# Signalling each group's edge sums by a drain of TensorE instead of by the last matmul, in all four graph layers of a fused GNN and expert network

## The reference, cut to what matters

```python
msg = table[src] * norm[:, None]                          # one row per edge, gathered by src
agg = jax.ops.segment_sum(msg, dst, num_segments=6250)    # summed per target node
```

## Time and profile before

| | us |
|---|---|
| runs of the kernel before | 5611.9 and 5638.83, median 5625.36 |
| span of the profiled execution | 5647.3 |
| granted TensorE clock, mean over the span | 0.835 |
| TensorE matmul, busy | 4017.9 |
| VectorE, busy | 3072.1 |
| GpSimd, busy | 2967.7 |
| ScalarE, busy | 1485.5 |

### The profile page before, as it was taken

One profiled execution on the slowest core, in us unless ns is written; L12 is line 12 of the kernel. 1 busy time (PEld: TensorE's weight loads), 2 busy tenths in 40 slices (PEclk: granted clock), 3 DMA queues, 4 the chain that ended last, 5 costly groups with the idle time before them and its releaser, 6 DMA issues.

```text
span 5647.3 us, 64923 instructions
## 1 busy us (share of the span) xinstructions
PE 4017.9 (71%) x21108; PEld 3177.4 (56%) x21109; DVE 3072.1 (54%) x7978; ACT 1485.5 (26%) x4028; POOL 2967.7 (53%) x3232
## 2 busy tenths in 40 slices
PE   7764555555546676777778977788776778785999
PEld 6653433334335466666666755666655666664766
DVE  7765645555447655555555565555546554443434
ACT  6502322232232222222223322222231111124221
POOL 7736466666656555555640016555556555543233
PEclk9987777776678777777779988899988998997999
DMA  2423433333333222222221013333333332225231
GB/s 89 122 68 93 118 96 97 96 96 96 97 89 87 78 80 79 80 80 80 82 67 34 20 60 87 89 92 90 90 102 97 102 93 84 83 77 176 69 104 54
DMA packets 272106, 489.99 MB, mean 87 GB/s; under 512 B 85684, under 2 KB 176805, under 8 KB 271635
## 3 DMA queue, kind: packets, MB, share of 16 engines
q0 software_dynamic: 139312, 377.94, 23.8%
q1 hardware_dynamic: 125336, 101.03, 5.9%
q10 hardware_dynamic: 7118, 6.83, 0.4%
HBM read 426.41 MB, written 62.17 MB: 87 GB/s over the span
## 4 chain that ended last, share of the span: by engine, by line
PE 39%; another core or an unknown queue 23%; DVE 22%; issue 10%; ACT 3%; DVEq 2%; POOL 1%; DMA 1%; ACTq 0%; SPq 0%; POOLq 0%
PE PSA L1020 11%; PE PSA L1164 5%; DVE ACC L2016 4%; PE PSA L1411 4%; PE PSA L1397 4%; PE PSA L1173 3%; PE PSA L1298 3%; PE PSA L1314 3%; DVE XIN L1989 2%; DVE XT L1989 2%; PE PSA L985 1%; PE PSA L979 1%; DVE WORK L2282 1%; PE PSA L1149 1%
## 5 line engine op out<-in xcount | busy, mean ns | idle before, releaser
L853 POOL DMA_INDIRECT WORK<-tab,SRC x2632 | 2522.8, 958 | 2146.8 <-issue 768.0
L2016 DVE TENSOR_TENSOR ACC<-ACC,PSA 64x256 f32 x1360 | 568.9, 418 | 1457.7 <-remote 959.4
L1020 PE MATMUL PSA<-WORK,XIN 128*128 128x256 f32 x3192 | 960.0, 454 | 458.0 <-ACT XIN L1491 341.5
L1020 PEld LDWEIGHTS PSA<-WORK,XIN 128*128 128x128 f32 x3192 | 711.0, 233 | 612.1 <-issue 492.5
L1020 PE MATMUL PSA<-WORK,XT 128*128 128x256 f32 x2072 | 594.5, 437 | 161.4 <-ACT XT L1491 85.4
L1020 PEld LDWEIGHTS PSA<-WORK,XT 128*128 128x128 f32 x2072 | 439.4, 222 | 248.9 <-issue 172.6
L1149 PE MATMUL PSA<-WORK 128*128 128x256 bf16 x784 | 161.6, 290 | 327.4 <-DVE WORK L2282 98.2
L1173 PE MATMUL PSA<-WORK,XT 128*128 128x42 f32 x832 | 153.8, 350 | 211.8 <-DVE WORK L1989 211.7
L1149 PEld LDWEIGHTS PSA<-WORK 128*128 128x128 bf16 x784 | 69.4, 104 | 379.8 <-issue 230.4
L1989 DVE TENSOR_TENSOR XIN<-PSA,DST 128x512 f32<-128x512 f32 x412 | 279.1, 679 | 2.5 <-DVE PSA L2323 1.4
L1173 PEld LDWEIGHTS PSA<-WORK,XT 128*128 128x128 f32 x832 | 145.8, 260 | 223.7 <-DVE WORK L1989 221.7
(11 more groups left out here) (492 smaller groups left out, 6899.0 us busy)
## 6 DMA issues: line engine op xcount, KB each, us to landing
WORK<-tab,SRC POOLq DMA_INDIRECT x2632
ACC<-in_L_ffn_w SPq DMA_DIRECT2D x16, 1024.0 KB
tab<-WORK SPq DMA_DIRECT2D x98, 128.0 KB
slots_x<-FILL SPq DMA_DIRECT2D x4, 2080.0 KB
ACC<-slots_x SPq DMA_DIRECT2D x8, 910.0 KB
tab<-ACC SPq DMA_DIRECT2D x49, 128.0 KB
WORK<-tab SPq DMA_DIRECT2D x49, 128.0 KB
before_y<-X SPq DMA_DIRECT2D x7, 896.0 KB
```

What stands on the lines that cost most here:

```text
L853: po.indirect_dma_start(out=rows[:, 0:width], out_offset=None, in_=tab[:, :], in_offset=bass.IndirectOffsetOnAxis(ap=SRC[:, c:c + 1].bitca ...
L1020: last = pe.matmul(PS[h][:, 0:D], chosen[:, j * P:(j + 1) * P], rows[:, 0:D], start=(j == 0), stop=(j == Q - 1))
L2016: return ve.tensor_tensor(rows, rows, PS[h][half, 0:D], ALU.add)
```

## The change

TensorE's loop over the groups no longer puts the increment of `s_p` on the last matmul of the product. It issues a `drain` behind the product, and the drain increments `s_p`. It does so for every group of all four layers. The rest of the queue of TensorE follows behind the drain as before, and nothing changes on another engine.

```diff
@@ -1194,7 +1194,8 @@
                         pe.wait_ge(s_free, 4 + BEGIN[1] + g - 2)
                     if layer >= 2 and g >= 2:
                         pe.wait_ge(s_free, 4 + BEGIN[layer] + g - 1)
-                    product(SEL[g % NS], rows_of(layer, g), bank_of(layer, g)).then_inc(s_p, 1)
+                    product(SEL[g % NS], rows_of(layer, g), bank_of(layer, g))
+                    pe.drain().then_inc(s_p, 1)
                     if layer == 3:
                         gate_steps(g)
                     if g in early:
```

## The result

The kernel before took 5625.36 us, the changed one 5788.95 us (median of 2 runs each, 5777.82 and 5800.09). The ratio is 1.0294, 95% interval 1.0218 to 1.0371: slower. The profiled execution has a span of 5776.1 us, 128.8 us over that of before.

The account below looks back on a forecast made before the run. A cycle of gather streams and held TensorE completions was taken to bound the kernel. Drains, 128 us, plus the queue behind held drains, 80 us, made 208 us over the 5625 us median: about 5835 us, range 5740 to 6040.

Parts of the forecast that it names:

- What bounds the kernel: In the four layers, gathers set 5.0 us a group; GpSimd's pauses and layer starts add 809 us, to 4209 us.
- The cycle of rows of gathers and late completions: GpSimd streams gathers, TensorE's signals stay out, slots fill up, GpSimd pauses, signals come, GpSimd starts again.
- Case (a): On TensorE, the drain too waits for held completions: its signal is as late as the matmul's, and the queue stands behind it.
- rival 1: The drain's signal is prompt, or its flush lets held ones out; sums come earlier: 5330 us, chance 0.32.
- First term: TensorE's queue: 0.35 us per drain, 92 us in layers 2 and 3, 36 in layers 0 and 1; together 128 us.
- Second term: TensorE work behind a held drain starts after release: 0.6 us per pause in layers 2 and 3, 80 us.
- Pauses: GpSimd's pauses keep their length, near 2.8 us in layers 2 and 3, but are more in number.
- rival 3: Far slower: each burst gives back one group only, one pause per group in layers 2 and 3: 6200 us, chance 0.08.
- Rival 2: No change: what the drain keeps back would have stood still anyway; drains cost some 40 us, 5665 us, chance 0.20.

Follow-up runs that it names:

- one and the same edit: GpSimd waits for its rows to land behind every second group of layers 1 to 3, against the kernel before: 0.9705 with completions held, 1.088 without.

## Why the prediction was right, and where it was not

The time was forecast at 5835 us and came at 5788.95; on its own terms, +208 us against +163.6 (medians), or +208.6 for the variant with a plain drain.

*What bounds the kernel: right, with a limit.* The cycle of rows of gathers and late completions is there in each profile in which before takes some 5650 us. The estimate that the gathers' pace without it would give 809 us less is borne out: without a hold the kernel before takes 5625.36 - 4728.96 = 896 us less, and in the changed kernel, which costs the same there, the four layers take 3409 us, 800 less than the 4209 of the earlier trace rows. That was not to be seen in the trace, which shows one execution in one condition.

*Case (a), a drain waits for the held completions: right.* The row of 680 drains up to 21.5 us and the pair at 3824.70 and 3824.73 show it; rival 1 has fallen. The Trainium skill, page "PSUM — Partial Sum Buffer", section "Engine vs sequencer instructions", has the drain wait until its engine is idle: by that rule, and the runs agree, its signal can't pass the matmuls'. The Trainium skill, page "Perfetto Trace Analysis", section "Sequencer-only Instruction (DRAIN, etc)", has the drain's update pushed by the sequencer. That brought no earlier sums here: VectorE's waits are 1316.8 us where they were 1349.2.

*First term, the drain itself, 128 us: the size was right and its place wrong.* The step predicted 0.35 us each, and the rows give 0.40. The step that failed is "in layers 2 and 3 the queue of TensorE is 78% busy and I take it whole": a high busy share doesn't put a queue on the path. Where nothing is held, TensorE is 92% busy in layer 2, and the 680 drains cost 1 us (1.0002), not 128.

*Second term, the queue behind a held drain, 80 us: right in kind, wrong in where.* For layers 0 and 1 the prediction said "for these two I take nothing". There the run with these layers alone measured 126 us, against 36 in all that I had given them, and some 90 of them are in layer 1. The rows of L1058, L1081 and L1173 are what I had named ("in layer 1 the moves of kept edges follow it") and not priced. In layers 2 and 3 the two terms made 172 us; 57 by stretches and 78 by the run with these layers alone are what came. The second term's 80 us would fit that by themselves, but no run splits the two terms within a hold.

So the total came out near by luck in part: in the runs by halves, 94 us too much in layers 2 and 3 met 90 too little in layers 0 and 1; in the changed kernel's own profile it was 115 too much and 34 too little.

*Pauses: right in length, nearly so in number.* In layers 2 and 3 GpSimd's waits for sums were 68 and 65, and the sum left their number as it was. After, in the same views:

```profile
POOL WORK L853 <- DVE ACC L2017: 211.7, 81, 5.7
```
```profile
POOL WORK L853 <- DVE ACC L2017: 192.3, 72, 4.3
```

That is 404.0/153 = 2.6 us each, and 20 more of them: rival 3, one pause per group, has fallen. Rival 2, no change, is what comes without the hold, for another reason than the one given: there no signal is held, and TensorE has slack.

## What to carry to other kernels

In this kernel a drain as such costs 0.40 us, which a queue with slack hides; what it can cost is everything that stands behind it while the engine's completions are late. So before a drain is put into a queue, list what follows it on that engine and ask how long after the work the waiter's wait really ends. And a kernel that is bound by a late signal should be timed in both conditions: one and the same edit gave 0.97 in one and 1.09 in the other.

## What the hardware showed that I had not expected

The same kernel before takes 5610 to 5674 us in three series and 4723 to 4736 us in two, with nothing in between. In the first, TensorE's completions come late, in layers 2 and 3 mostly some 2 us after the end of a row of gathers; in the second the add stands 0.2 us behind the matmul in the midst of the row, while the gathers take as long (958 ns, and 960 ns in the row below, from the changed kernel's page) and the packets too.

```profile
L853 POOL DMA_INDIRECT WORK<-tab,SRC x2632 | 2527.6, 960 | 1288.9 <-issue 779.1
```

It is nearly TensorE alone that is late. In the trace of before, 816 of its 2163 recorded signals come over 1 us behind the end of their matmul, but only 8 of ScalarE's 1180 and 49 of VectorE's 4421; in the kernel with the plain drain and no hold it is 10 of TensorE's 2389. The end of a row of gathers explains part of it: of the sum signals of before that are over 1 us late, 49 of 57 in layer 2 and 34 of 55 in layer 3 come 1.5 to 2.4 us after a gather's end. In layer 0 the median is 3.6 us after it, and in layer 1 only 24 of 71 fall there and 20 come while a gather runs. Since a matmul's end is modelled, the traces don't tell whether the matmul itself ends late or only its report.

One chip number occurs in both kinds of series. If it is the same piece, the hold isn't a fixed property of the chip; I can't tell. What holds the completions, and what makes the condition come and go, stays open.

The granted clock follows: 0.73, 0.75, 0.91 and 0.90 in the layers with the hold, 0.81, 0.85, 0.98 and 0.96 without, as TensorE stands still less. So part of what the hold costs is likely paid in slower matmuls; it was not measured apart. With the drain at the end of the group a single case shows it, the product behind an idle of 4.00 us, which took 3.44 us at a clock of 0.50 in place of 1.89.
